# Decoder layer on one core: values of the first 128 keys split by side into two banks, transposes moved behind scores

## The reference

```python
# x: (2, 2048, 512), ctx: (2, 154, 512), all float32
x = layernorm(x + linear_attention(x))            # 8 heads, no softmax
q, k, v = x @ W_q.T, ctx @ W_k.T, ctx @ W_v.T      # with biases; 16 heads of 32
scores  = q @ k.T / sqrt(32), masked keys -> -1e9
x = layernorm(x + (softmax(scores) @ v) @ W_o.T + b_o)
xr, xk = mixes of x with the row before it (mu_r, mu_k)
x = layernorm(x + sigmoid(xr @ W_r) * (relu(xk @ W_k)**2 @ W_v))
```

## Time and profile before

| | |
|---|---|
| median of 3 runs | 915.81 us (915.44 to 916.83) |
| the profiled execution's own time | 914.96 us |
| its span, first to last instruction | 912.9 us |
| TensorE busy | 896.7 us (98%) |
| VectorE, ScalarE, GpSimd busy | 695.6, 556.5, 521.8 us |
| instructions | 23290 |

### The profile page before, as it was taken

One profiled execution on the slowest core, in us unless ns is written; L12 is line 12 of the kernel. 1 busy time (PEld: TensorE's weight loads), 2 busy tenths in 40 slices (PEclk: granted clock), 3 DMA queues, 4 the chain that ended last, 5 costly groups with the idle time before them and its releaser, 6 DMA issues.

```text
span 912.9 us, 23290 instructions
## 1 busy us (share of the span) xinstructions
PE 896.7 (98%) x8774; PEld 749.0 (82%) x8774; DVE 695.6 (76%) x1994; ACT 556.5 (61%) x1667; POOL 521.8 (57%) x505
## 2 busy tenths in 40 slices
PE   8999999999999999999999999999999999999997
PEld 7867766787788888888878888888888888888886
DVE  6688566578877878787877878787877777787775
ACT  7555236858675756575856666666665757575631
POOL 1045015759666666666675757566676767665420
PEclk9999999999999999999999999999999999999999
DMA  8792020113000001012101010101010100100001
GB/s 296 245 271 58 24 94 2 43 36 136 9 25 31 25 25 31 24 32 82 32 24 32 24 32 25 32 25 32 25 32 24 31 26 12 44 2 24 2 24 46
DMA packets 32332, 46.54 MB, mean 51 GB/s; under 512 B 3806, under 2 KB 16606, under 8 KB 32094
## 3 DMA queue, kind: packets, MB, share of 16 engines
q1 hardware_dynamic: 28622, 37.99, 12.8%
q10 hardware_dynamic: 3600, 7.08, 2.3%
HBM read 34.10 MB, written 9.70 MB: 48 GB/s over the span
## 4 chain that ended last, share of the span: by engine, by line
PE 75%; DVE 4%; POOL 4%; issue 4%; ACT 1%; POOLq 0%; ACTq 0%
PE dense L92 19%; PE dense L94 17%; PE dense L93 17%; PE turned L1664 5%; PE turned L1686 5%; PE scores L1650 4%; PE dense L1540 2%; PE turned L1668 1%; PE turned L1540 1%; POOL row_inv L1442 1%; POOL weight L1450 1%; PE scores L1546 1%; DVE mix_k_raw L1204 1%; PE dense L1557 0%; POOL prob_rest L1449 0%
## 5 line engine op out<-in xcount | busy, mean ns | idle before, releaser
L1442 POOL TENSOR_TENSOR row_inv<-row_sum,minus_one 128x4 f32<-128x4 f32 x128 | 152.6, 1192 | 190.1 <-ACT prob L818 190.0
L818 ACT ACTIVATE prob<-prob,row_min 128x154 f32<-128x154 f32 x512 | 209.6, 416 | 39.8 <-DVE row_min L1160 39.8
L1450 POOL TENSOR_TENSOR weight<-prob,row_inv 128x512 f32<-128x512 f32 x128 | 148.0, 1156 | 0.0
L1160 DVE CUSTOM_DVE_ANT_0 prob<-scores,mask_add 128x154 f32<-128x154 f32 x512 | 127.8, 312 | 4.0 <-PE scores L1650 3.7
L826 ACT ACTIVATE prob_t<-turned 128x512 f32<-128x512 f32 x128 | 76.0, 594 | 84.6 <-PE turned L1664 83.8
L818 ACT ACTIVATION_READ_ACCUMULATOR prob<-prob,row_min 128x1 f32 x512 | 98.3, 192 | 0.0
L1664 PE MATMUL turned<-ident,weight 128*128 128x128 f32 x512 | 76.9, 272 | 3.4 <-DVE o_t_lo L1167 3.0
L1664 PEld LDWEIGHTS turned<-ident,weight 128*128 128x128 f32 x512 | 61.2, 139 | 17.9 <-issue 6.3
L92 PE MATMUL dense<-mix_k_hi,ffn_wk_hi 128*128 128x256 f32 x256 | 75.3, 294 | 0.0
L92 PE MATMUL dense<-xt_hi,cross_wq_hi 128*128 128x256 f32 x256 | 75.2, 294 | 0.0
L94 PE MATMUL dense<-mix_k_hi,ffn_wk_lo 128*128 128x256 f32 x256 | 72.3, 283 | 0.0
(11 more groups left out here) (276 smaller groups left out, 2684.7 us busy)
## 6 DMA issues: line engine op xcount, KB each, us to landing
x_rows<-x_rows SPq DMA_DIRECT2D x32, 256.0 KB, 4.6
xt_raw<-x_cols SPq DMA_DIRECT2D x16, 512.0 KB, 3.8
out<-gate_then_y SPq DMA_DIRECT2D x15, 512.0 KB, 2.8
mask_in<-mask SPq DMA_DIRECT2D x16, 154.0 KB, 2.3
cross_wv<-cross_wv SPq DMA_DIRECT2D x2, 512.0 KB, 6.6
cross_wk<-cross_wk SPq DMA_DIRECT2D x1, 1024.0 KB, 9.3
self_wv<-self_wv ACTq DMA_DIRECT2D x1, 1024.0 KB, 7.3
self_wk<-self_wk ACTq DMA_DIRECT2D x1, 1024.0 KB, 9.6
```

The source lines that it names most:

```text
L818: m = act.activation(keys, keys, ACT.Exp, bias=row_min[:, buf, t, h:h + 1], scale=-1.0, accum_out=row_sum[:, buf, t, h:h + 1])
L1160: m = dve.tensor_tensor_reduce(exp_slot(n, u)[:, i * CTX:(i + 1) * CTX], s_bank[:, h, t * CTX:(t + 1) * CTX], mask_add[n % 2][:, t, :], -S ...
L1442: pool.tensor_tensor(row_inv[:, buf, t, :], row_sum[:, buf, t, :], minus_one[:], ALU.pow).then_inc(*p_inv.up)
L1450: pool.tensor_tensor(first, early, inv_early, ALU.mult).then_inc(*p_norm.up)
```

## The change

Values: the first 128 keys are no longer cut into two pieces. Each head's block of `prob_t` holds all 128 keys; rows 0 to 63 (side 0) and 64 to 127 (side 1) are one matmul each, over all 256 tokens at once, and write bank 0 and bank 1. The 26 rest keys are added per tile into the bank of their side. A new VectorE step o_take sums the two banks into `ot_raw` in SBUF; o_high and o_low read that, and the waits that freed the banks with o_low now ask for o_take (`ot_sum`). `t_bank` and the other bank of `turned` change places.

Buffers: four probability tiles (two head groups, two tiles) take the place of the three `prob` and two `weight` slots; weigh multiplies in place. The difference of x2 has a tile of its own, there is one mask_in instead of two, `v_first` is half as large, and the copies that fill it are fewer.

Order: transposes(n,1,0) and transposes(n,3,0) stand directly behind scores, with the product that stood between them behind; x2_turn(f,1) goes ahead of x1_turn(a,1); rounds 0 and 1 are written anew on VectorE, ScalarE and TensorE. On VectorE o_take stands where o_low stood or earlier, and normalise(2, f) moves behind the next masked_min.

```diff
+            def o_take(n, g):
+                dve.wait_ge(*pv_mm.at(n, g + 1))
+                if n:
+                    dve.wait_ge(*o_mm.at(n - 1))
+                dve.tensor_reduce(ot_raw[:, g, :], value.rearrange("p s n -> p n s"), mybir.AxisListType.X, ALU.add).then_inc(*ot_sum.up)
...
             def o_low(n, g):
                 dve.wait_ge(*ot_hi_ok.at(n, g + 1))
-                dve.tensor_tensor(by_t(ot_lo[:, g, :]), value, by_t(f32(ot_hi[:, g, :])), ALU.subtract).then_inc(*ot_lo_ok.up)
+                dve.tensor_tensor(ot_lo[:, g, :], ot_raw[:, g, :], f32(ot_hi[:, g, :]), ALU.subtract).then_inc(*ot_lo_ok.up)
...
             def o_high(n, g):
-                act.wait_ge(*pv_mm.at(n, g + 1))
-                if n:
-                    act.wait_ge(*o_mm.at(n - 1))
-                act.activation(by_t(ot_hi[:, g, :]), value, ACT.Copy).then_inc(*ot_hi_ok.up)
+                act.wait_ge(*ot_sum.at(n, g + 1))
+                act.activation(ot_hi[:, g, :], ot_raw[:, g, :], ACT.Copy).then_inc(*ot_hi_ok.up)
...
             def transposes(n, g, t):
...
                 elif n + g:
-                    pe.wait_ge(*ot_lo_ok.at(n, g))
+                    pe.wait_ge(*ot_sum.at(n, g))
...
-                for piece in range(PIECES + 1):
-                    for t in range(TPG):
-                        for h in range(HPG):
-                            rows = slice(side_of(h, t) * SIDE_ROWS, (side_of(h, t) + 1) * SIDE_ROWS)
-                            cols = slice((g * HPG + h) * DK, (g * HPG + h + 1) * DK)
-                            if piece < PIECES:
-                                sta, block = v_first[rows, b, piece, cols], piece * PIECES + h // SIDES
-                            else:
-                                sta, block = v_rest[rows, b, g, h * DK:(h + 1) * DK], HPG
-                            m = pe.matmul(value[h * DK:(h + 1) * DK, t, :], sta, pt[rows, block, t * P:(t + 1) * P],
-                                          start=(piece == 0), stop=(piece == PIECES), skip_group_check=True)
+                for side in range(SIDES):
+                    rows = slice(side * SIDE_ROWS, (side + 1) * SIDE_ROWS)
+                    for h in range(HPG):
+                        cols = slice((g * HPG + h) * DK, (g * HPG + h + 1) * DK)
+                        pe.matmul(value[h * DK:(h + 1) * DK, side, :], v_first[rows, b, cols], pt[rows, h, :],
+                                  start=True, stop=False, skip_group_check=True)
+                for t in range(TPG):
+                    for h in range(HPG):
+                        side = place_of(h, t) // SIDES
+                        rows = slice(side * SIDE_ROWS, (side + 1) * SIDE_ROWS)
+                        m = pe.matmul(value[h * DK:(h + 1) * DK, side, t * P:(t + 1) * P],
+                                      v_rest[rows, b, g, h * DK:(h + 1) * DK], pt[rows, HPG, t * P:(t + 1) * P],
+                                      start=False, stop=True, skip_group_check=True)
...
             def x2_turn(n, t):
...
-                    pe.wait_ge(*ot_lo_ok.at(n + 1, 2))
+                    pe.wait_ge(*ot_sum.at(n + 1, 2))
...
-            def fold_m0_high(cs):
-                pe.wait_ge(*fu_ok.at(0, KT + cs[-1] + 1))
+            def fold_m0_high():
+                pe.wait_ge(*fu_high.at(0))
...
                 values(n, 0)
                 scores(n, 2)
+                transposes(n, 1, 0)
                 y_product(a, 1)
-                transposes(n, 1, 0)
+                transposes(n, 1, 1)
                 r_product(e, 0)
-                transposes(n, 1, 1)
                 r_product(e, 1, early)
...
                 values(n, 1)
                 scores(n, 3)
+                x2_turn(f, 1)
                 x1_turn(a, 1)
-                x2_turn(f, 1)
                 k_product(e, 1)
...
                 scores(a, 0)
+                transposes(n, 3, 0)
                 v_product(e, 0)
-                transposes(n, 3, 0)
-                v_product(e, 1, early)
                 transposes(n, 3, 1)
-                v_product(e, 1, late_half)
+                v_product(e, 1)
                 values(n, 3)
```

More of the change, by code:

```diff
@@ L155, in prologue @@
     placements = []
[L156 to L170 removed]
+    for b in range(B):
+        row = b * CTX
+        while row < b * CTX + P:
+            n, to = min(b * CTX + P - row, P - row % P), row - b * CTX
+            placements.append((v_first[to:to + n, b, :], v_raw[row % P:row % P + n, row // P, :]))
+            row += n
+    for j in range(HPG):
+        for b in range(B):
+            row = b * CTX + P
+            while row < (b + 1) * CTX:
+                n = min((b + 1) * CTX - row, P - row % P)
+                for side in range(SIDES):
+                    to = side * SIDE_ROWS + j % SIDES * DK + row - b * CTX - P
                     placements.append((
@@ L589, in main_tiles @@
     tile["q"] = mem.place("q", [P, HG, GT])
-    tile["prob"] = mem.place("prob", [P, EXP_SLOTS, GK])
-    tile["weight"] = mem.place("weight", [P, WEIGHT_SLOTS, HPG * P])
+    for i in range(2):
+        tile[f"prob{i}"] = mem.place(f"prob{i}", [P, TPG, GK])
     for i in range(2):
@@ L599, in main_tiles @@
     tile["x2t"] = mem.place("x2_t", [P, KT, 1 + GT])
+    tile["diff"] = mem.place("diff", [P, KT, GT])
     tile["gate"] = mem.place("gate_then_y", [P, TPG, D])
@@ L1266, in dve_program @@
             dve.wait_ge(*setup.at(0))
-            for n in range(-1, LAST):
+            for t in range(TPG):
+                y_finish(0, t)
+            normalise(1, 0, x1[0])
+            take_t(1)
+            for t in range(TPG):
+                x1t_low(0, t)
+            make_mask(0)
+            take_t(2)
+            weight_low("ffn_wk")
+            masked_min(0, 0, 0)
+            masked_min(0, 0, 1)
+            take_t(3)
+            masked_min(0, 1, 0)
+            masked_min(0, 1, 1)
+            x_low(1)
+            take_kv()
+            dve.wait_ge(*fkv_mm.at(0))
+            carry(0)
+            y_finish(1, 0)
+            y_finish(1, 1)
+            o_take(0, 0)
+            normalise(1, 1, x1[1])
+            masked_min(0, 2, 0)
+            masked_min(0, 2, 1)
+            make_mask(1)
+            x1t_low(1, 0)
+            o_take(0, 1)
+            x1t_low(1, 1)
+            o_low(0, 0)
+            bias_u(0, 1)
+            masked_min(0, 3, 0)
+            masked_min(0, 3, 1)
+            o_low(0, 1)
+            u_high()
+            bias_u(2, 3)
+            u_low()
+            o_take(0, 2)
+            masked_min(1, 0, 0)
+            masked_min(1, 0, 1)
+            o_low(0, 2)
+            take_c()
+            o_take(0, 3)
+            masked_min(1, 1, 0)
+            o_low(0, 3)
+            masked_min(1, 1, 1)
+            o_finish(0, 0)
+            o_finish(0, 1)
+            o_take(1, 0)
+            masked_min(1, 2, 0)
+            normalise(2, 0, x2[0])
+            y_finish(2, 0)
+            o_low(1, 0)
+            masked_min(1, 2, 1)
+            y_finish(2, 1)
+            normalise(1, 2, x1[0])
+            make_mask(2)
+            x1t_low(2, 0)
+            o_take(1, 1)
+            x1t_low(2, 1)
+            add_one(0, 1, 2)
+            masked_min(1, 3, 0)
+            masked_min(1, 3, 1)
+            o_low(1, 1)
+            difference(0)
+            blend(0, "k")
+            blend(0, "r")
+            carry(1)
+            o_take(1, 2)
+            masked_min(2, 0, 0)
+            masked_min(2, 0, 1)
+            k_mix_low(0)
+            o_low(1, 2)
+            add_one(3)
+            for n in range(2, LAST):
                 a, f, e = n + 1, n - 1, n - 2
@@ L1377, in dve_program @@
                 o_finish(LAST - 1, t)
-            o_low(LAST, 0)
+            o_take(LAST, 0)
             masked_min(LAST, 2, 0)
             normalise(2, LAST - 1, x2[(LAST - 1) % 2])
+            o_low(LAST, 0)
             k_square(LAST - 2, 1)
@@ L1383, in dve_program @@
             k_low(LAST - 2, 1)
-            o_low(LAST, 1)
+            o_take(LAST, 1)
             masked_min(LAST, 3, 0)
@@ L1387, in dve_program @@
             masked_min(LAST, 3, 1)
+            o_low(LAST, 1)
             blend(LAST - 1, "k")
+            v_finish(LAST - 2, 0)
+            o_take(LAST, 2)
+            k_mix_low(LAST - 1)
             o_low(LAST, 2)
-            k_mix_low(LAST - 1)
-            v_finish(LAST - 2, 0)
             blend(LAST - 1, "r")
@@ L1395, in dve_program @@
             k_square(LAST - 1, 0)
+            o_take(LAST, 3)
+            k_low(LAST - 1, 0)
             o_low(LAST, 3)
-            k_low(LAST - 1, 0)
             normalise(3, LAST - 2, y3)
@@ L1843, in pe_program @@
             scores(1, 2)
+            transposes(1, 1, 0)
             y_product(2, 1)
-            transposes(1, 1, 0)
+            transposes(1, 1, 1)
             fold_m(2, early)
-            transposes(1, 1, 1)
+            x2_turn(0, 0)
             fold_m(2, late_half)
-            x2_turn(0, 0)
             x1_turn(2, 0)
```

(2 more changed lines are left out.)

358 lines of the change are left out of this document (133 added, 225 removed).

## The result

The changed kernel takes 945.24 us (median of 4 runs, 944.33 to 945.32), the kernel before on the same chip 916.13. The ratio is 1.0315, with a 95% interval of 1.0298 to 1.0333: slower, as predicted, but by 29 us where 12 were predicted, and outside the range.

The account below looks back on a forecast made before the run. TensorE's queue in its written order was taken to bound the kernel. Values -3.8, A +3.4, B +9.5, C +3.1 and first rounds 0 gave +12.2 us, so 928.0 us; own range 920 to 936, 8 in 10 within 914 to 942.

Parts of the forecast that it names:

- A: transposes(n,1,0) behind scores(n,2) wait for o_take: 0.24 us a round, 3.4 us over rounds 2 to 15.
- B: x2_turn(f,1) behind scores(n,3) waits for o_take, queued behind x1t_low(a,0): 0.73 us a round, 9.5 us in 13 rounds.
- C: transposes(n,3,0) behind scores(a,0) wait for o_take: 0.24 us a round, 3.1 us in 13 rounds, 0.3 us slack.
- The reduce: o_take on VectorE, summing 2 x 256 PSUM values per partition, 64 times: 0.685 us each, bounds 0.42 and 1.37.
- The four predicted terms: Per steady round: values -0.24, A +0.24, B +0.73, C +0.24 us, sum +0.97.
- rival 1: Reduce takes 1.37 us (955 us in all), or VectorE is late at C (934.5); chance of 936 or more: 0.15.
- rival 2: Reduce takes only 0.42 us, A and C vanish, B is 0.46: 918 us; chance of 914 to 920: 0.13.
- rival 3: Values get much cheaper, each row half having its own bank: 21 us saved, 910.7 us; chance of under 914: 0.12.
- The values: 32 passes instead of 48 in each of 64 groups: 0.81 us for 0.87, saving 0.06 each, 3.8 us in all.
- The first rounds: Rounds 0 and 1: round 0 near zero, round 1 +1.3 us, 0.92 taken away in round 2; together about 0.

Follow-up runs that it names:

- new_order_own_list: The change's TensorE and ScalarE order with VectorE's list of own_order_to_end, except v_finish(13,0) stays ahead of o_take(15,2): 922.68 us, ratio 1.0076.
- low3_first: Changed kernel with o_take(f,3), masked_min(n,1,0) and o_low(f,3) moved ahead of v_finish(e-1,1) on VectorE: 935.69 us, ratio 1.0218.
- bias_later: Changed kernel with GpSimd's add_bias(a) moved behind r_mix_low(f) in rounds from 2 on: 936.12 us, ratio 1.0224.
- old_order_all: Changed kernel with TensorE's and ScalarE's order of before in rounds 2 to 15, and v_finish(13,0) behind o_low(15,2) on VectorE: 920.39 us, ratio 1.0056.
- own_order_to_end: old_order_all with VectorE's list rearranged for the sum, last round included, and v_finish(13,1) in two parts: 912.02 us, ratio 0.9961.
- turn_behind_x1: Changed kernel with x1_turn(a,1) put back ahead of x2_turn(f,1) on TensorE, ScalarE's two copies likewise: 929.89 us, ratio 1.0165.
- new_order_alone: Kernel before with only the change's TensorE order of rounds 2 to 14, ScalarE's order to match: 929.28 us, ratio 1.0150.
- old_tensor_order: Changed kernel with TensorE's order of before at all three places in rounds 2 to 14, ScalarE's order to match: 921.68 us, ratio 1.0069.

## Why the prediction was wrong

**What held.** The three places, the engine that each waits for, and their sizes: A 0.31 us for 0.24, B 0.64 for 0.73, and C 0.40 for 0.24, of which 0.31 is its floor (new_order_own_list). The reduce takes 0.686 us for 0.685. The four predicted terms come to 1.11 us a round where 0.97 was forecast, and the products give 0.20 back. Of the rivals, the dear reduce of rival 1, the short one of rival 2 and the cheap values of rival 3 all fell. The time lies where rival 1 put it (936 or more), but not by its causes: the reduce isn't dear, and C is late by less than 0.1 us.

**What held by luck.** The values take 0.81 us for the 0.81 forecast, but the saving isn't where the prediction looked. With half as many passes v_first still takes 0.43 to 0.46 us; the 0.06 come in v_rest (0.41 us to the scores before, 0.35 to 0.39 now), whose number of passes is the same. The first rounds were put at zero as a sum of larger parts: up to round 2 the loss is 0.04 us because round 0 is 0.83 us shorter and round 1 is 0.75 longer (1.3 was forecast). The reading of stalls was wrong too. "the four largest are 2.00, 0.98, 0.92 and 0.29 us, 4.2 together, and all lie before 236 us" leaves out these two of the kernel before, in rounds 2 and 6:

```profile
245.43 0.63 PE L1540 MATMUL turned<-ident,x 128*128 128x128 f32 x4 [0.81 <-DVE o_t_lo L1167]
...
464.76 0.47 PE L92 MATMUL dense<-m_hi,xt_hi 128*128 128x512 f32 x1 [1.12 <-DVE x L1173]
```

Two more, of 1.05 and 1.32 us, stand in the prologue. The stall at 464.76 is most of the 1.3 us by which the round with the batch change is longer. It is gone in the changed kernel (no run shows why), which is a good part of why round 6 cost only 1.4 us.

**The first step that failed:** "o_high and o_low now read SBUF; their users are the output products of a later round, so they are covered". The later round is the next one, and for g = 3 the user stands close. TensorE in the kernel before, values(n,3), the transposes behind k_product, and o_product(f,0):

```profile
358.18 0.67 PE L1686 MATMUL turned<-prob_t,v_first 64*32 64x128 f32 x32
...
362.77 0.60 PE L1664 MATMUL turned<-ident,weight 128*128 128x128 f32 x4
363.12 0.48 PE L92 MATMUL dense<-cross_wo_hi,o_t_hi 128*128 128x512 f32 x1
```

In these 5 us VectorE now has v_finish(e-1,1), the reduce and a masked_min, where o_low(f,3) had stood directly behind v_finish. VectorE in the changed kernel, the second instruction of v_finish and o_low(f,3), and GpSimd beside it:

```profile
364.38 1.42 DVE L1210 SCALAR_TENSOR_TENSOR gate_then_y<-gate_then_y,x 128x512 f32<-128x512 f32 x1
...
368.40 0.42 DVE L1150 TENSOR_TENSOR o_t_lo<-o_t_raw,o_t_hi 128x256 fp32r<-128x256 f32 x1
```

```profile
364.20 1.04 POOL L1453 TENSOR_TENSOR prob<-prob,row_inv 128x512 f32<-128x512 f32 x1
```

The same instruction of v_finish in the kernel before:

```profile
359.08 0.69 DVE L1231 SCALAR_TENSOR_TENSOR gate_then_y<-gate_then_y,x 128x512 f32<-128x512 f32 x1
```

o_low(f,3) ends at 368.82, and TensorE goes on at 368.88. Counted from the start of values(n,3), o_low starts 2.0 us later than in the kernel before: some 1.3 by the reduce and the masked_min, and 0.73 because the second instruction of v_finish now runs under a multiplication of GpSimd. This is a collision as well, and by an estimate from the rows neither part alone makes the wait. In the kernel before, o_low ended at 361.51 and o_product started at 363.12; less 0.06 for the handover and 0.1 by which TensorE is now sooner through values and transposes, the cover is about 1.4 us, and 1.3 would stay within it. No run moves this multiplication alone. Cost: 0.59 us a round by the trace. low3_first gives 9.5 us in all, but 3.2 of them are the wait of the second step, so its 9.5 and the 9.1 of bias_later can't be added. I had asked what follows the reduce and not what follows each instruction that the reduce and the rewritten list push back.

**The second:** "VectorE's load, 64 x 0.685 = 44 us, costs nothing by itself: 10 us of slack per round against 2.7", and for B "the queue behind the wait is x1_turn(a,1), k_product and all that follows". The slack is an average. Between x1t_low(a,0) and k_mix_low VectorE had no idle time before either, 12 us long, and the kernel before had 0.9 us to spare behind it (o_low(n,2) starts at 351.12, and k_mix_low ends at 350.22). What stands behind B on TensorE releases not only TensorE's own work: x1_turn(a,1) releases add_bias on GpSimd, and by its lateness the collisions rose. The row that warned was there (one instruction between 1.22 and 2.06 us). The prediction named the collision and its victim (o_low, 1 us more), put it in a sentence beside the sum, and expected it at C; it came 1.03 us long, and hit q_product(a,1) first. Cost: 0.64 us in 11 rounds and 0.08 at C, 9.1 us in all by bias_later.

The Trainium skill (SBUF — State Buffer, Who interferes with whom) says that a VectorE instruction with two SBUF inputs contends with a GpSimd instruction that reads SBUF, and that tensor_reduce never does. The runs agree: o_low takes 0.41 to 0.42 us alone and 1.45 beside add_bias, while the 64 reduces lie between 671 and 692 ns in the changed kernel, those beside a GpSimd multiplication included. But the reduce reads PSUM and has no SBUF input, so no run here tests a tensor_reduce that reads SBUF.

**The third,** a term left out: the last two rounds. From values(14,0) to the end the terms make about 1.0 us (one round of 0.97, and A of round 15 less its values); 6.2 came. o_product(14,0) waits 1.30 us and transposes(15,1,0) 1.27, by the brackets, and two more wait 0.88 each. One of these is o_product(15,0), waiting for o_low, where the prediction had said that a k_product of 3 us covers it. There the products that cover a wait are fewer, and v_finish, k_square and the reduce stand close together in VectorE's list; that this is the cause is argued from the list. The last-round edits of old_order_all and own_order_to_end together gave 1.3 + 2.6 = 3.9 us of it back.

The order of the failures by size: rounds 2 to 13 were 23.4 us instead of 12 x 0.97 = 11.6, mostly by the first two steps, and the end 5.2 us more than its terms, by the third.

## What to carry to other kernels

An engine's slack per round says nothing about a stretch in which it doesn't rest: follow its list from the last idle time before the change to the next idle time behind it, and ask of every instruction in it who waits for it. When TensorE stalls, ask what its late instructions release on every engine; here a start moved by 1 us put two instructions that read SBUF on top of each other and cost more than the stall. What counts is not how long such instructions take in sum but whether someone waits for the one that is hit. And read a loss from start to start, since the bracket shows only the part that isn't overlapped.

## What the hardware showed unexpectedly

- The same 256-value subtraction with both operands in SBUF took 0.41 us alone and 1.45 us beside a GpSimd addition of 2.41 us. Four blends took 1.78 us or 2.46 us with the place of GpSimd's multiplications.
- The extra time follows the overlap. In the cases that follow, a VectorE instruction with both inputs in SBUF that starts while GpSimd adds or multiplies takes longer by the time that GpSimd still needs, less 0.12 to 0.15 us. For o_low, 1.16 us of overlap gave 1.03 more (changed kernel), 1.24 gave 1.12 (bias_later) and 0.19 gave 0.06 (turn_behind_x1). For the second instruction of v_finish, 0.87 gave 0.73 (changed kernel), 0.64 gave 0.50 (new_order_alone) and 0.50 gave 0.36 (old_tensor_order). For k_mix_low of the kernel before, 0.98 gave 0.84.
- Over the whole kernel, VectorE's same instructions took 732.3, 728.0, 722.6, 713.7 or 709.2 us, by nothing but order (changed kernel, bias_later, low3_first, turn_behind_x1, own_order_to_end).
- A stall between transposes and a product costs about 0.25 us more than its bracket (0.34 in brackets, 0.59 from start to start), one between scores and transposes 0.06 to 0.07 more (0.22 and 0.28).
- 32 passes of values instead of 48, with the same columns per tile, took 0.81 us instead of 0.87. Both row halves wrote each bank before, but never in the same partitions: tile 0 and tile 1 of a head are computed by different halves, and they lie in different banks. Now each half has a bank of its own, and v_first takes the same 0.46 us. So sharing a bank in that way cost nothing here, and the runs don't say what two halves in the same partitions of one bank would cost.
